# Attention and feed-forward on one core: three probability blocks of four key tiles per step instead of six of two, and GpSimd summing four key tiles

## What is computed

```
qkv    = x @ w_qkv.T + b_qkv
scores = q @ k.T / sqrt(32) + causal
out    = softmax(scores) @ v
x      = layernorm(x + out @ w_out.T + b_out)
hidden = relu((x @ sign(up).T) * up_scale)
x      = layernorm(x + (hidden @ sign(down).T) * down_scale * output_scale)
```

## Time and profile before

| | us |
|---|---|
| median of 3 runs | 797.18 |
| lowest, highest | 793.76, 798.38 |
| profiled execution, its time | 801.23 |
| its span | 799.5 |
| TensorE busy | 746.0 (93% of the span) |
| VectorE, GpSimd, ScalarE busy | 456.0, 345.9, 323.2 |

### The profile page before, as it was taken

How to read it: one execution, slowest core, us unless ns; L and a number is a source line. 1 busy time by engine, 2 the same in 40 slices (tenths; PEclk the granted TensorE clock), 3 DMA queues, 4 the chain that set the end, 5 groups by cost and what they waited for, 6 DMA issues and landing times.

```text
span 799.5 us, 11694 instructions
## 1 busy us (share of the span) xinstructions
PE 746.0 (93%) x4048; PEld 509.6 (64%) x4048; DVE 456.0 (57%) x1086; ACT 323.2 (40%) x631; POOL 345.9 (43%) x479
## 2 busy tenths in 40 slices
PE   6899899999999999999989897999999999999994
PEld 4687655655556455555554453588778877878882
DVE  3276386676766767758576662433277329433614
ACT  5111355555555655545555556532231223221220
POOL 4441456364553555544527534362244234323333
PEclk9999899999999999999997997999999999999998
DMA  6966263525545344344467440413002101000101
GB/s 233 311 166 184 68 178 114 146 81 144 156 112 157 95 134 145 92 145 124 130 188 219 145 162 5 155 43 119 14 14 105 27 14 39 14 1 2 52 1 52
DMA packets 44619, 85.71 MB, mean 107 GB/s; under 512 B 4880, under 2 KB 13584, under 8 KB 44432
## 3 DMA queue, kind: packets, MB, share of 16 engines
q1 hardware_dynamic: 35536, 79.72, 33.1%
q10 hardware_dynamic: 9024, 5.24, 2.3%
HBM read 55.33 MB, written 29.36 MB: 106 GB/s over the span
## 4 chain that ended last, share of the span: by engine, by line
PE 75%; DVE 15%; issue 4%; ACT 2%; DMA 2%; POOL 2%; ACTq 0%; SPq 0%; POOLq 0%; DVEq 0%
PE ps_heads L1013 9%; PE ps_unit L946 9%; PE ps_proj L906 8%; DVE heads_sb L805 7%; PE ps_proj L1056 7%; PE ps_score L983 6%; PE ps_score L1073 6%; PE ps_unit L1029 6%; PE ps_unit L1056 5%; PE ps_sum L1007 5%; PE ps_heads L1073 3%; PE ps_sum L1073 3%; DVE maxes L783 2%; PE ps_sum L991 2%; DVE heads_sb L807 2%
## 5 line engine op out<-in xcount | busy, mean ns | idle before, releaser
L681 ACT ACTIVATE probs<-ps_score 128x512 f32<-128x512 f32 (+3 forms) x360 | 170.8, 490 | 180.1 <-PE ps_score L983 171.3
L779 DVE CUSTOM_DVE_ANT_0 ps_unit<-ps_unit,causal 128x128 f32<-128x128 f32 (+3 forms) x256 | 121.9, 512 | 77.0 <-PE ps_unit L946 74.3
L625 POOL TENSOR_TENSOR hid_low<-hid_raw,hid_high 128x512 fp32r<-128x512 f32 x64 | 85.0, 1328 | 174.6 <-DVE hid_high L856 171.5
L946 PE MATMUL ps_unit<-stack 96*128 96x512 f32 (+3 forms) x384 | 134.4, 364 | 10.9 <-DVE maxes L783 4.3
L983 PE MATMUL ps_score<-stack 98*128 98x512 f32 (+2 forms) x360 | 134.9, 383 | 7.5 <-ACT probs L681 6.0
L594 POOL TENSOR_SCALAR_AFFINE_SELECT probs<-probs 128x128 f32<-128x128 f32 x256 | 73.9, 294 | 153.6 <-ACT probs L681 150.9
L946 PEld LDWEIGHTS ps_unit<-stack 96*128 96x128 f32 x384 | 72.6, 193 | 57.3 <-issue 17.4
L856 DVE CAST hid_high<-hid_raw 128x512 fp32r<-128x512 f32 x64 | 27.1, 424 | 131.1 <-ACT hid_raw L736 130.9
L783 DVE TENSOR_REDUCE maxes<-ps_unit 128x1 f32<-128x512 f32 x128 | 80.7, 684 | 26.0 <-PE ps_unit L946 25.6
L983 PEld LDWEIGHTS ps_score<-stack 98*128 98x128 f32 x360 | 69.3, 195 | 40.6 <-ACT probs L681 23.9
L1013 PE MATMUL ps_heads<-probs,v_rows 128*32 128x512 f32 (+3 forms) x768 | 84.5, 511 | 5.1 <-DVE heads_sb L807 3.3
(11 more groups left out here) (184 smaller groups left out, 1208.1 us busy)
## 6 DMA issues: line engine op xcount, KB each, us to landing
stack<-qk_parts SPq DMA_DIRECT2D x96, 256.0 KB, 4.7
qk_parts<-parts SPq DMA_DIRECT2D x32, 512.0 KB, 2.7
v_all<-h_even ACTq DMA_DIRECT2D x16, 256.0 KB, 3.4
v_rows<-v_all SPq DMA_DIRECT2D x8, 512.0 KB, 4.5
heads_t<-heads_sb SPq DMA_DIRECT2D x16, 256.0 KB, 2.6
raw<-up_w SPq DMA_DIRECT2D x8, 512.0 KB, 3.6
x_tile<-x_rows SPq DMA_DIRECT2D x16, 256.0 KB, 5.0
raw<-down_w SPq DMA_DIRECT2D x8, 512.0 KB, 3.8
```

What stands on the lines that cost most here:

```text
L625: nc.gpsimd.tensor_tensor(hid[1][:, (HM * s + n) % 3, :], hid_raw[:, n % 2, :], hid[0][:, (HM * s + n) % 3, :].bitcast(FP32), ALU.subtract ...
L681: nc.scalar.activation(probs[:, (NP * s + n) % RING, 0:width], score_bank(s, n)[:, off:off + width], ACT.Exp, scale=SCALE).then_inc(s_exp, 1)
L779: nc.vector.tensor_tensor_reduce(ps_unit[n % 3][:, 0:width], ps_unit[n % 3][:, 0:width], causal[:, HALF - width:], 1.0, NEG, ALU.add, ALU.max,
L946: nc.tensor.matmul(ps_unit[n % 3][:, 0:width], stack[s % 2][0:96, 1, f, h, i % 4 * P:(i % 4 + 1) * P], stack[s % 2][0:96, 0, c, h, 0:width ...
```

## The change

In steps 0 to 5 the twelve groups of probabilities times values stand in three blocks of four, at 19.6, 36 and 52, and the ring grows from 14 to 20 tiles to hold the tiles longer. GpSimd adds all four undiagonal key tiles (twelve additions a step, at 21.7 to 36), and one `sum_added` of four matmuls at 51.9 takes the place of two. In steps 6 and 7 GpSimd adds nothing, and the sums of these groups run on TensorE. The slots of maxima and projections move: the eviction of the projection of step s+2's keys goes from slot 44.05 to 52.1 and its fill from 49.2 to 57.4, the eviction of (1, 2) from 13.05 to 10.15, and the first shift transpose from before the block at 36 to behind it. From step 1 on, a projection takes its low weight part last. In the changed kernel lines from 594 on stand up to six lower: L906 is L912 there, L946 is L952, L957 is L963, L983 is L989, L1007 and L1013 are L1013 and L1019, L660 and L654 are L666 and L660.

```diff
-RING = 14
+RING = 20
...
-PAIRED = [13, 13, 19.6, 19.6, 28, 28, 36, 36, 44, 44, 52, 52]
-PAIRED_NORM = [19.7, 19.71, 19.72, 19.73, 52.05, 52.06, 52.07, 52.08]
+FOURS = [19.6] * 4 + [36] * 4 + [52] * 4
+FOURS_NORM = [19.7, 19.71, 19.72, 19.73, 52.05, 52.06, 52.07, 52.08]
...
-MAXIMA = ([10.2 + 0.55 * u for u in range(5)] + [13.4 + 0.55 * u for u in range(11)]
-          + [25.2 + 0.6 * u for u in range(5)] + [28.4 + 0.7 * u for u in range(27)])
-
-
-BLOCK = [(1, 2, 4.2, 0.72, 13.05, 15.8, 18.5), (1, 3, 13.3, 0.5, 19.65, 22.4, 24.8),
-         (2, 0, 22, 1.1, 36.05, 38.8, 41.3), (2, 1, 36.3, 0.6, 44.05, 46.8, 49.2)]
+MAXIMA = [10.2 + 0.57 * u for u in range(16)] + [25.6 + 0.66 * u for u in range(32)]
+
+
+BLOCK = [(1, 2, 4.3, 0.5, 10.15, 13, 15.5), (1, 3, 10.7, 0.74, 19.65, 22.4, 24.8),
+         (2, 0, 21, 1.2, 36.05, 38.8, 41.3), (2, 1, 38.3, 1.1, 52.1, 54.9, 57.4)]
...
-NA = 2 * GH
+NA = 3 * GH
+ADDING = STEPS - 2
...
-            if g < FIRST_ADD or g >= LAST_ADD:
+            if g < FIRST_ADD or g >= LAST_ADD or s >= ADDING:
                 put(t + at, "sum", s, g)
-        for a in range(2):
-            for h in range(GH):
-                put(t + 25.6 + 8 * a + 0.01 * h, "add", s, GH * a + h)
-            put(t + (33, 41)[a], "sum_added", s, a)
...
+        if s < ADDING:
+            for a in range(NA):
+                put(t + 21.7 + 1.3 * a, "add", s, a)
+            put(t + 51.9, "sum_added", s)
...
-            put(t + 35.9, "shift", s + 1, 0)
+            put(t + 36.02, "shift", s + 1, 0)
...
-    pairs = sb(left, "pairs", [P, GH, HALF], FP32)
+    added = sb(left, "added", [P, GH, HALF], FP32)
...
-                    k = NP * s + GH * (FIRST_ADD + n // GH * 2) + n % GH
-                    pool.wait_ge(s_exp, k + GH + 1)
-
-                    wait(pool, s_used, NA * s + n - GH + 1)
-                    nc.gpsimd.tensor_tensor(pairs[:, n % GH, :], probs[:, k % RING, :], probs[:, (k + GH) % RING, :],
-                                            ALU.add).then_inc(s_add, 1)
+                    h = n % GH
+                    k = NP * s + GH * (FIRST_ADD + 1) + n
+                    pool.wait_ge(s_exp, k + 1)
+                    if n < GH:
+
+                        wait(pool, s_used, GH * s - GH + h + 1)
+                        other = probs[:, (k - GH) % RING, :]
+                    else:
+                        pool.wait_ge(s_add, NA * s + n - GH + 1)
+                        other = added[:, h, :]
+                    nc.gpsimd.tensor_tensor(added[:, h, :], other, probs[:, k % RING, :], ALU.add).then_inc(s_add, 1)
...
-                    (wp, xp), c = PARTS[m // DC], m % DC
+                    (wp, xp), c = PARTS[m // DC if m < DC or s == 0 else 3 - m // DC], m % DC
...
-                        pe.wait_ge(s_add, NA * s + GH * n + h + 1)
-                        nc.tensor.matmul(ps_sum[rows, :], ones[:, :], pairs[:, h, :], start=(n == 0), stop=False,
+                        pe.wait_ge(s_add, NA * s + NA - GH + h + 1)
+                        nc.tensor.matmul(ps_sum[rows, :], ones[:, :], added[:, h, :], start=True, stop=False,
                                          tile_position=(0, h * HD)).then_inc(s_used, 1)
...
-    nc = bacc.Bacc("TRN2", target_bir_lowering=False, num_devices=1)
+    nc = bacc.Bacc("TRN2", target_bir_lowering=False, num_devices=1, dynamic_dma_scratch_size=1024)
```

More of the change, by code:

```diff
@@ L140, in plan @@
             put(t + n, "score", s, n)
-        paired = s < STEPS - 2
-        for g, at in enumerate(PAIRED if paired else ALONE[s % 2]):
+        fours = s < STEPS - 2
+        for g, at in enumerate(FOURS if fours else ALONE[s % 2]):
             put(t + at, "pv", s, g)
-            if g < FIRST_ADD or g >= LAST_ADD:
+            if g < FIRST_ADD or g >= LAST_ADD or s >= ADDING:
                 put(t + at, "sum", s, g)
-        for a in range(2):
-            for h in range(GH):
-                put(t + 25.6 + 8 * a + 0.01 * h, "add", s, GH * a + h)
-            put(t + (33, 41)[a], "sum_added", s, a)
-        for q, at in enumerate(PAIRED_NORM if paired else ALONE_NORM[s % 2]):
+        if s < ADDING:
+            for a in range(NA):
+                put(t + 21.7 + 1.3 * a, "add", s, a)
+            put(t + 51.9, "sum_added", s)
+        for q, at in enumerate(FOURS_NORM if fours else ALONE_NORM[s % 2]):
             put(t + at, "norm", s, q)
@@ L276, in build @@
         s_rc = sem("row_sum_inverted")
-        s_add = sem("prob_pairs_added")
-        s_used = sem("prob_pairs_used")
+        s_add = sem("probs_added")
+        s_used = sem("added_probs_used")
         s_norm = sem("heads_normalized")
@@ L677, in _ @@
                     wait(act, s_pv, NP * s + n - RING + 1)
-                    k = n - RING - GH * FIRST_ADD
-                    if 0 <= k < 2 * NA:
-                        act.wait_ge(s_add, NA * s + k // (2 * GH) * GH + k % GH + 1)
+                    s0, k = (NP * s + n - RING) // NP, (n - RING) % NP - GH * FIRST_ADD
+                    if 0 <= s0 < ADDING and 0 <= k < GH * (LAST_ADD - FIRST_ADD):
+                        act.wait_ge(s_add, NA * s0 + (k if k < GH else k - GH) + 1)
                     nc.scalar.activation(probs[:, (NP * s + n) % RING, 0:width], score_bank(s, n)[:, off:off + width],
@@ L696, in _ @@
                     else:
-                        if n == 14:
+                        if n == 15:
                             act.wait_ge(s_pv, NP * STEPS)
@@ L1013, in _ @@
                         mm = nc.tensor.matmul(ps_heads[rows, at:at + width], v_rows[:, s % 2, j, rows], tile, **args)
-                        if FIRST_ADD <= n < LAST_ADD:
+                        if s < ADDING and FIRST_ADD <= n < LAST_ADD:
                             mm.then_inc(s_pv, 1)
```

## The result

| | us |
|---|---|
| before, median of 4 runs | 796.41 (793.76 to 798.38) |
| after, median of 4 runs | 847.45 (843.65 to 848.58) |
| ratio after to before | 1.0636, 95% interval 1.0596 to 1.0675 |
| profiled execution after, its span | 848.58, 846.9 |

The change makes the kernel slower by 51 us. Of the spans, 799.5 before and 846.9 after, the difference is 47.4 us; the forecast of 44.4 was made against that execution. The 3.7 us between 47.4 and 51 lie in the executions: the profiled one of before took 801.23, 4.8 over its median, that of the change 1.1 over its own.

The account below looks back on a forecast made before the run. The keys' chain from eviction to fill to u0 was taken to have no slack. 5 x (6.05 + 1.5) + 8.4 - 0.35 - 1.4 = +44.4 us on 801.23 gave 845.6, or 842 against the median; range 818 to 862.

Parts of the forecast that it names:

- E: The moment in a step at which TensorE starts score 4 behind the block at 52.
- u0: TensorE's unit that needs the keys' fill; predicted at E + 12.6 us, from 11.9 to 13.7.
- E to S: First piece of a step: the late eviction and fill lengthen it from 17.0 to 24.6 us, +7.6.
- S: The moment in a step at which TensorE starts score 20 behind the block at 19.6.
- S to the block at 36: Second piece of a step: two blocks leave it, VectorE's maxima then set it at 13.5 us, -3.4.
- its end to E: From the block at 36 to the next E: taken as 0 change, bounds -0.5 and +0.9 us.
- The wait before u0: TensorE, otherwise there at E + 6.4, idles 6.2 us a step for the keys' fill.
- 1.5 us of clock: Work at the lower clock after the new wait, taken as 1.5 us a step, between nothing and 4.
- The rival at 834: The fill is late, but TensorE's clock holds: +36.9 us, 834 us; chance 0.20.
- The store at nothing: On SyncE the heads' store now precedes the fill but is due while the keep is under way: no cost.
- the gain of 1.4 us for the last steps: Steps 6 and 7: four-group sums add 1.0 us each; step 7's GpSimd wait and lower clock go: together -1.4.
- the blocks' gain could come through: Rival: u0 stays and VectorE doesn't bound the second piece; six steps of 2.1 us, -12.7, 784 us; chance 0.05.

Follow-up runs that it names:

- short maxima: Sixteen of VectorE's forty-eight maxima a step read 128 of 512 columns, against the changed kernel with both evictions mended (795.36 us): 788.53 us, ratio 0.9897.
- the third kernel: Changed kernel with the keys' eviction, keep and fill back at their old slots and projection (1, 3) starting at 12.3, spaced 0.58: 795.36 us, ratio 0.9979.
- the last one tried: Against the third kernel: later units from slot 37.55, eviction of (2, 0) at 32.6 ahead of the block at 36, projection (2, 1) from 36.1: 796.76 us.

## Why the prediction was right, and where its sizes were off

**The mechanism.** It stands as predicted: the eviction starts behind the exponential of score 4, the projection waits 1.74 us (2 were said), the fill is issued 6.2 us behind E (6 to 8), u0 waits in six places. The waits before u0 are 4.4 to 6.7 us, three of the six below the 5 to 7 that were named. That one line carries it is shown from both sides: put alone into the kernel before it costs 60 us, taken back from the change it returns 43.

**The pieces of a step.**

| piece | before | predicted | after, step 2 |
|---|---|---|---|
| E to S, with the clock's term | 17.0 | 24.6 + 1.5 | 25.8 (mean of five 26.2) |
| S to the block at 36 | 16.9 | 13.5 | 13.5 (13.49 to 13.50 in all five) |
| block at 36 | 1.85 | 3.7 | 3.6 |
| its end to E | 15.4 | 15.4 | 15.7 |
| step | 51.1 | 58.65 | 58.56 (mean of five 58.95) |

u0 came 12.05 to 12.89 us behind E; 12.6 was taken out of 11.9 to 13.7. The 0.3 us in the last piece is the wait of u33 behind the shift transpose, 0.74 us, less the boundaries; the bound for it was 0.9.

**The wait before u0** was too large in the prediction: 31.4 us in six places, 5.2 each, instead of 6.2. TensorE did not reach u0 at E + 6.4 but at E + 7.7 in step 2 (213.50 less 4.51), since the projections behind the first wait ran at the lower level too. In step 3 the clock held there, and TensorE reached u0 at E + 6.1. The windows of step 2:

```profile
204.00:208.00 4.00, 4.00 (x13) 3.37 (x13) 2.33 (x5) 1.62 (x4) 1.69 (x4) 0.57 0.50 196
208.00:212.00 4.00, 0.99 (x6) 0.59 (x4) 0.00 (x0) 2.17 (x5) 2.15 (x4) 0.86 0.81 194
212.00:216.00 4.00, 2.50 (x8) 2.24 (x9) 1.47 (x6) 0.39 (x1) 0.29 (x1) 0.50 0.43 149
216.00:220.00 4.00, 4.00 (x19) 3.40 (x18) 3.28 (x14) 1.11 (x4) 1.18 (x4) 0.78 0.82 222
```

The low stretch of the first line comes ahead of the wait for the fill, which absorbs it, since u0 is set by the fill; the one behind u0, 0.50 and 0.78, is on the path. So of the two waits a step the prediction's 1.5 us of clock belongs to the second, and measured it is 1.9. It was taken between nothing and 4, with 1.7 in the nearer of the two rows. The reason given for the choice, a VectorE nearly as slow as TensorE behind u0, does not hold: at full clock VectorE is busy 8.10 of the 11.83 us there. That the size came out close is in part luck. From u0 to S the granted clock is 0.78 to 0.87 in steps 1 to 5, and the half clock stands behind u0 in all six places. The rule cited in the prediction (the Trainium skill, "TensorE: Matmul & The Clock Gate", section "HAM oscillation — how this bites in real kernels") agrees with this trace: each of the six steps restarts at half clock behind its wait. The rival at 834, in which the clock holds, falls with the measured clock.

**What would be TensorE's own limit between S and the block at 36** was mis-sized: "some 10 us" is 12.0 with short maxima, 0.55 of it waits. VectorE bounds that piece, as said, but takes back 1.5 us and not 3.5. The sum is not touched by it.

**The store at nothing.** In the change this holds: keep to fill is 2.65 us with the store between them. The reason given for it holds too: the store is issued at E + 5.1, 1.1 us ahead of the fill, which follows the keep by as much as a keep takes to land (2.65 us, median 2.6). That margin hangs on the late eviction. Once the eviction is early, the same store costs 28 us; it was the expectation of that experiment that left the store out, not the prediction.

**The ends.** Steps 0, 6 and 7 come to 8.2 us (0.4 and 7.8) against a forecast of 6.65. u0 of step 6 is 12.2 us behind E, 8.0 later than before; from u0 to the end the change takes 397.3 us and the kernel before 397.5. So the gain of 1.4 us for the last steps is not seen there. No run isolates that term: it stays open.

**The rivals.** No added sum was waited for: the last addition ends at 244.54 in step 2, the sum starts at 254.24. That the blocks' gain could come through, 784 us, is refuted for this order even without its waits (795.36). Against the kernel with GpSimd's part alone (0.9922) the new order with both evictions mended (0.9979) is slower by 0.6%, 4.5 us. So the change is three things: summing four key tiles on GpSimd, with the ring of 20 and the low parts last, -6 us; three long blocks in place of six short ones, with the slots that go with them, +4 to +5; and two evictions too late for what waits on them, +52, 43 of it the keys' and 9 that of (1, 2). The parts hold in this order only: put alone into the kernel before, the keys' eviction costs 60, and the wait behind (1, 2) shows only once the fill no longer covers it.

## What to carry to other kernels

When work is gathered into longer blocks, what used to run under the blocks that go must be followed to its first consumer, through every in-order queue: here 0.8% was to be had, and a transfer that came eight microseconds later in each step cost eight times that. Move the tables of such a plan one at a time, for the part that pays (GpSimd's sums) needed no new order at all. In an issue queue ask of each transfer not only what it delays but what it stands behind.

## What was not expected of the hardware

The clock fell in places without a long wait. In the kernels with three blocks and a mended eviction, TensorE's waits ahead of the block at 52 are 0.33 to 0.41 us and 0.16 us, and yet the added sum behind them takes 1.94 us instead of 1.06 in two steps of six in the third kernel and in all six of the last one tried. In the kernel with six blocks and GpSimd's part, which has a block at 44 in between, the clock is 1.00 at that place in every step. In the third kernel such a step is about 1.2 us longer (51.7 against 50.5); the last one has no step at full clock to compare. What decides between the two was not tried by itself, and stays open.
